# A graph network on one core: deeper rings in the edge sort, three banks of sums and fewer waits in the layers

## What is computed

```python
for l in range(3):
    X = einsum('ne,ref->rnf', out, weights[l])        # one product per edge type
    msg = X[edge_type, dst] + biases[l][edge_type]
    out = segment_sum(msg, src)                        # relu after layers 0 and 1
x = layernorm(x + out)
alpha = beta * cos(x[row], x[col])                     # row, col: the edges and loops
x = layernorm(x + softmax over each row's edges of alpha, times x[col])
```

## Time and profile before

| quantity | before |
|---|---|
| median of 3 runs | 4264.41 us |
| the profiled execution | 4270.03 us |
| its span, first to last instruction | 4268.3 us |
| mean granted TensorE clock | 0.862 of full speed |
| TensorE matmul busy | 3096.6 us (73%) |
| VectorE busy | 2434.5 us (57%) |
| ScalarE busy | 857.6 us (20%) |
| GpSimd busy | 2752.9 us (64%) |
| instructions | 55641 |

### The profile page before, as it was taken

The page is one execution under the profiler, slowest core; times in us unless marked ns, Lnnn a source line. Parts: engine busy times, 40 slices in busy tenths (PEclk is TensorE's granted clock), DMA queues, the critical chain, the costliest instruction groups (busy, mean ns, idle before and its releaser), DMA issues.

```text
span 4268.3 us, 55641 instructions
## 1 busy us (share of the span) xinstructions
PE 3096.6 (73%) x13925; PEld 1821.7 (43%) x13926; DVE 2434.5 (57%) x9103; ACT 857.6 (20%) x1992; POOL 2752.9 (64%) x2839
## 2 busy tenths in 40 slices
PE   7799957676776678667667667777775655656998
PEld 4455424333433334333334333344333434434776
DVE  9888855554555556555554554465554333335999
ACT  2599801001001000001001001001000000002665
POOL 0777777777777772777777777647777777772000
PEclk9899979999899997999998998898997555556999
DMA  4100013333433437333333333553433222224564
GB/s 157 42 2 2 2 45 83 78 71 80 80 72 78 81 72 175 70 72 76 83 72 74 84 74 71 71 175 76 83 72 85 53 53 53 53 53 76 185 192 141
DMA packets 377130, 343.02 MB, mean 80 GB/s; under 512 B 263666, under 2 KB 327722, under 8 KB 376712
## 3 DMA queue, kind: packets, MB, share of 16 engines
q0 software_dynamic: 90368, 165.49, 19.7%
q1 hardware_dynamic: 83112, 113.25, 8.0%
q10 hardware_dynamic: 203360, 60.73, 5.9%
HBM read 232.12 MB, written 107.13 MB: 79 GB/s over the span
## 4 chain that ended last, share of the span: by engine, by line
POOL 63%; issue 21%; PE 9%; DVE 5%; DMA 2%; ACT 1%; SPq 0%; POOLq 0%; DVEq 0%; ACTq 0%
POOL region L817 55%; POOL scattered_edges L800 8%; PE ps L958 2%; PE ps L929 2%; PE ps L986 2%; DMA region<-x_of_type,arrays 1%; DVE region L340 1%; DVE region L608 1%; PE ps L961 1%; PE ps L919 1%; DVE region L580 0%; PE ps L908 0%; DVE arrays L368 0%; DVE arrays L379 0%; DVE region L599 0%
## 5 line engine op out<-in xcount | busy, mean ns | idle before, releaser
L817 POOL DMA_INDIRECT region<-x_of_type,arrays x2520 | 2415.7, 959 | 918.9 <-issue 764.9
L908 PE MATMUL ps<-oh,region 128*128 128x102 f32 x5040 | 1261.3, 340 | 725.9 <-DMA region<-x_of_type,arrays 707.0
L441 DVE TENSOR_SCALAR oh<-iota_w,arrays 128x102 f32<-128x102 f32 x2528 | 724.3, 290 | 1703.7 <-PE ps L908 1701.4
L919 PE MATMUL ps<-region 128*128 128x510 f16 x4200 | 1402.0, 410 | 346.8 <-issue 195.8
L908 PEld LDWEIGHTS ps<-oh,region 128*128 128x128 f32 x5040 | 1000.1, 228 | 1454.9 <-DMA region<-x_of_type,arrays 1281.2
L919 PEld LDWEIGHTS ps<-region 128*128 128x128 f16 x4200 | 434.5, 113 | 549.8 <-issue 527.2
L505 DVE TENSOR_TENSOR region<-region,ps 128x102 f32 x2520 | 646.1, 256 | 3.6 <-issue 3.2
L1048 ACT COPY region<-ps 128x510 f32<-128x510 f32 x155 | 89.8, 579 | 2482.8 <-PE ps L919 2482.3
L800 POOL DMA_INDIRECT scattered_edges<-region x304 | 332.8, 1095 | 207.0 <-DVE ends L398 109.3
L887 PE MATMUL ps<-region 128*128 128x420 f16 x2016 | 362.6, 342 | 24.9 <-ACT region L1025 24.9
L1025 ACT ACTIVATE region<-region 128x128 f16<-128x128 f16 x1008 | 348.8, 394 | 39.7 <-DVE region L418 29.6
(11 more groups left out here) (173 smaller groups left out, 1486.4 us busy)
## 6 DMA issues: line engine op xcount, KB each, us to landing
region<-x_of_type,arrays POOLq DMA_INDIRECT x2520, 2.6
edge_counts<-region ACTq DMA_DIRECT2D x155, 255.0 KB
arrays<-edge_counts SPq DMA_DIRECT2D x40, 960.0 KB, 5.0
x_of_type<-region SPq DMA_DIRECT2D x50, 576.0 KB, 3.9
edge_absent<-region ACTq DMA_DIRECT2D x155, 127.5 KB
region<-edge_absent SPq DMA_DIRECT2D x40, 480.0 KB, 4.4
x_of_type<-x0st SPq DMA_DIRECT2D x51, 192.0 KB, 1.8
scattered_edges<-region POOLq DMA_INDIRECT x304
```

What stands on the lines that cost most here:

```text
L441: ins = nc_.tensor_scalar(oh[:, t % U, 0:RB], iota_r, rowf[:, t % NT:t % NT + 1], None, ALU.is_equal)
L817: pool.indirect_dma_start(out=grow[:, t % GR, :], out_offset=None, in_=xt, in_offset=bass.IndirectOffsetOnAxis(ap=gix[:, t:t + 1], axis=0) ...
L908: mm = pe.matmul(ps[:, 6 + n % 2, t * RB:(t + 1) * RB], grow[:, u % GR, :], oh[:, u % U, 0:RB], start=True, stop=True)
L919: mm = pe.matmul(ps[:, c, 0:CW], cl[:, q % CR, c * P:(c + 1) * P], cr[:, q % CR, :], start=False, stop=False, skip_group_check=True)
```

## The change

In the sort the rings get `KR` = 28 places, in a larger stretch of `region` that is free by then, and `s_put` is raised once per `KS` = 14 columns; VectorE and ScalarE wait on it only every 14 columns. In the layers, the sums of four tiles go to three banks in turn instead of two, the tiles' one-hots lie in a ring of 12 (`ohr`, now in `region`) instead of 8, and the keys' one-hots in a ring of 8 instead of 5. TensorE reads the thresholds of five columns at once, and waits once per column, ahead of bank 0, for all five refilled banks. The last 12 one-hots past the end, which nobody uses, are no longer made. What is computed, and every compute instruction else, is the same.

```diff
-KR = 4
+SUMS = 3
+OH = 12
+KR = 28
+KS = 14
-    CR = 5
+    CR = 8
+    CL = 5
-        used[0] = NK * ET // 2
+        used[0] = max(GR * D, NP) + NP
+        ohr = part(OH * P).rearrange("p (u d) -> p u d", u=OH)
-            dve.sem_inc(s_add, 2 * SLOTS)
+            dve.sem_inc(s_add, SUMS * SLOTS)
             # the sort, VectorE (ScalarE's wait changes alike)
-                if t >= KR:
-                    dve.wait_ge(s_put, t - KR + 1)
+                if t >= KR and t % KS == 0:
+                    dve.wait_ge(s_put, (t - KR) // KS + 1)
-            dve.wait_ge(s_put, EP)
+            dve.wait_ge(s_put, EP // KS)
-                ins = nc_.tensor_scalar(oh[:, t % U, 0:RB], iota_r, ...
+                ins = nc_.tensor_scalar(ohr[:, t % OH, 0:RB], iota_r, ...
-            for u in range(U):
+            for u in range(OH):
                 one_hot(u)
...
-                    one_hot(first + i * BODY + u + U)
+                    if first + i * BODY + u + OH < NT * L:
+                        one_hot(first + i * BODY + u + OH)
-                    dve.wait_ge(s_add, i * BODY + (first + u + 2 * SLOTS))
+                    dve.wait_ge(s_add, i * BODY + (first + u + SUMS * SLOTS))
-                    nc_.tensor_tensor(h, h, ps[:, 6 + n % 2, t * RB:(t + 1) * RB], ALU.add).then_inc(s_add, 1)
+                    nc_.tensor_tensor(h, h, ps[:, 5 + n % SUMS, t * RB:(t + 1) * RB], ALU.add).then_inc(s_add, 1)
             # TensorE in the sort
-                mm.then_inc(s_put, 1)
+                if t % KS == KS - 1:
+                    mm.then_inc(s_put, 1)
             # TensorE in the layers
-                    mm = pe.matmul(ps[:, 6 + n % 2, ...], grow[:, u % GR, :], oh[:, u % U, 0:RB],
+                    mm = pe.matmul(ps[:, 5 + n % SUMS, ...], grow[:, u % GR, :], ohr[:, u % OH, 0:RB],
                         if c == 0:
-                            ready = values_of(pe, b7, k, CG * (MB - 1) + 1, 1)[0]
+                            if q % CL == 0:
+                                ready = values_of(pe, b7, k // CL, CG * (MB - 1) + 1, CL)
                             pe.wait_ge(s_co, k + 1)
-                        if c % 2 == 0:
-                            reg_wait(pe, s_cz, ready + min(c + 1, CG - 1))
-                        mm = pe.matmul(ps[:, c, 0:CW], cl[:, q % CR, c * P:(c + 1) * P], cr[:, q % CR, :],
+                            reg_wait(pe, s_cz, ready[q % CL] + (CG - 1))
+                        mm = pe.matmul(ps[:, c, 0:CW], cl[:, k % CR, c * P:(c + 1) * P], cr[:, k % CR, :],
```

More of the change, by code:

```diff
@@ L77, in gnn_program @@
     assert all(b * JOINT_MUL >> BLOCK_SHIFT == b // JB for b in range(NB))
-    assert CP <= REST and EP % U == 0 and U == 2 * KR and HW <= 512 and NT <= 1 << DIGIT
-    assert BODY == GR and GR % U == 0 and BODY % U == 0 and U == 2 * SLOTS and ET <= KW and NT % SLOTS == 0
+    assert CP <= REST and EP % KR == 0 and KR % KS == 0 and HW <= 512 and NT <= 1 << DIGIT
+    assert BODY == GR and GR % U == 0 and BODY % OH == 0 and BODY // SLOTS % SUMS == 0 and NT // SLOTS % SUMS == 0 and U == 2 * SLOTS and ET <= KW and NT % SLOTS == 0
     assert R * NP < 1 << ROW_BIT and RB <= P and ROW_BIT + 7 <= 2 * DIGIT and NB % JB == 0 and PAD_ROW <= NP
@@ L95, in gnn_program @@
     CB = 10
-    CR = 5
+    CR = 8
+    CL = 5
     CTURNS = -(-NT // CB)
     CQ = CTURNS * CB
-    assert (L - 1) * TURNS < CTURNS < L * TURNS and CB % CR == 0 and CQ + CR < KW
+    assert (L - 1) * TURNS < CTURNS < L * TURNS and CB % CL == 0 and CQ + CR <= KW
     PARTS = [[] for _ in range(BODY)]
@@ L440, in one_hot @@
             def one_hot(t):
-                ins = nc_.tensor_scalar(oh[:, t % U, 0:RB], iota_r, rowf[:, t % NT:t % NT + 1], None, ALU.is_equal)
+                ins = nc_.tensor_scalar(ohr[:, t % OH, 0:RB], iota_r, rowf[:, t % NT:t % NT + 1], None, ALU.is_equal)
                 if t % SLOTS == SLOTS - 1:
@@ L501, in take_tiles @@
                             cell_hots(i * CB + (CB * TURNS * l + q + CR - 1))
-                    dve.wait_ge(s_add, i * BODY + (first + u + 2 * SLOTS))
+                    dve.wait_ge(s_add, i * BODY + (first + u + SUMS * SLOTS))
                     h = hA[:, bass.ds(bs[t], RB)]
-                    nc_.tensor_tensor(h, h, ps[:, 6 + n % 2, t * RB:(t + 1) * RB], ALU.add).then_inc(s_add, 1)
+                    nc_.tensor_tensor(h, h, ps[:, 5 + n % SUMS, t * RB:(t + 1) * RB], ALU.add).then_inc(s_add, 1)
             for l in range(L):
                 if l:
-                    dve.wait_ge(s_add, NT * l + 2 * SLOTS)
+                    dve.wait_ge(s_add, NT * l + SUMS * SLOTS)
                     for n in range(XN):
@@ L907, in use_tiles @@
                         pe.wait_ge(s_add, i * BODY + (first + u + SLOTS))
-                    mm = pe.matmul(ps[:, 6 + n % 2, t * RB:(t + 1) * RB], grow[:, u % GR, :], oh[:, u % U, 0:RB],
+                    mm = pe.matmul(ps[:, 5 + n % SUMS, t * RB:(t + 1) * RB], grow[:, u % GR, :], ohr[:, u % OH, 0:RB],
                                    start=True, stop=True)
@@ L941, in _ @@
             pe.wait_ge(s_cz, CG + CG * MB)
-            pe.wait_ge(s_add, NT * L + 2 * SLOTS)
+            pe.wait_ge(s_add, NT * L + SUMS * SLOTS)
             turn(lambda b: hA[:, b * P:(b + 1) * P])
@@ L1021, in _ @@
                 act.wait_ge(s_hot, t + 1)
-                if t >= KR:
-                    act.wait_ge(s_put, t - KR + 1)
+                if t >= KR and t % KS == 0:
+                    act.wait_ge(s_put, (t - KR) // KS + 1)
                 for d in range(2):
```

## The result

The changed kernel has a median of 4239.87 us (4237.43 to 4242.11, 4 runs), against 4264.88 us (4263.59 to 4267.21) for the kernel before, measured in turn with it. The ratio is 0.9941, with a 95% interval from 0.9923 to 0.9958. The forecast was 4247.4 us, its range 4233 to 4271; the change is 25 us where 17 were forecast. The profiled execution took 4240.06 us, its span is 4238.3 us.

The account below looks back on a forecast made before the run. The prediction took GpSimd's row of indirect DMAs to bound the kernel, in the sort's scatter and the layers' gathers. Its terms, -22 + 3 + 2 = -17 us against 4264.41, gave 4247.4 us, with a range of 4233 to 4271.

Parts of the forecast that it names:

- What bounds the kernel: Whole kernel: GpSimd's indirect DMAs, 304 in the sort and 840 per layer; the scatter decides the sort's end.
- TensorE in the sort: 0.713 us per column stays: Sort, TensorE: one signal per 14 columns buys nothing; 504 columns keep ending at about 523.3 us.
- GpSimd freed by bursts, d = 0.04: Sort: GpSimd's wait d per issue within VectorE's bursts is 0.04 us; last scatter starts at about 510, against 544.19.
- The cap: End of sort: TensorE's half becomes the limit, L452 starts at 526 instead of 549.41, -23 us; -22 taken.
- The rule of the Trainium skill: Sort, against the step: each issue held for a whole burst, +203 us, 4472 us; chance 0.03 for full blocking.
- The four casts: Before the sort's columns: an issue took 2.36 us, until 0.12 us after the last cast; cited for the full blocking.
- The layers' rhythm, +3: Layers: contact with VectorE, 0.018 us per gather issue, may shift its phase; bounds -38 and +38 us, +3 taken.
- The end of layer 0, +2: End of layer 0: the single wait for all five banks delays the last tiles, +2 us.
- The sum: Whole kernel: -22 (sort) + 3 (layers' rhythm) + 2 (end of layer 0) = -17 us, 4247.4 us forecast.

Follow-up runs that it names:

- run with 310 columns: Changed kernel with 310 columns scattered by GpSimd and 498 placed by TensorE, instead of 304 and 504: 4237.79 us, ratio 0.9924 to the kernel before.
- run with the layers' part alone: Changed kernel with the sort's part taken back (ring of 4, a signal per column): 4265.99 us against 4269.40 for the kernel before, ratio 0.9992.
- six kernels named above: Kernel before; it with the sort's part alone, that with signals per 1, 2 or 4 columns; it with a fifth matmul: first to last gather 3323.1 to 3326.4 us.
- three kernels: Layers' part alone, the changed kernel, and it with 310 scattered columns: 3318.6, 3319.7 and 3321.3 us from layer 0's first gather to layer 2's last.
- columns of 0.89 us: Kernel before with a fifth matmul per column of the sort into a bank that nobody reads: 4337.60 us.
- last runs: Kernel before, changed kernel and it with 310 columns again, on one chip: 5137.34, 5117.56, 5119.41 us; changed kernel with short key comparisons, two chips: 5119.48, 5112.86 us.

## Why the prediction was right, point by point

- **What bounds the kernel.** Right. The layers' gathers did not move by more than 1.8 us in any layer, although TensorE was idle by other amounts and its mean granted clock fell from 0.862 to 0.825. The scatter was the end of the sort, and TensorE's half is now.
- **TensorE in the sort: 0.713 us per column stays.** Right: 155 matmuls in 27.82 us, so (27.82 - 0.34) / 154 = 0.178 us each.
- **GpSimd freed by bursts, d = 0.04.** The outcome is right: with work waiting at VectorE, GpSimd's issue falls to 0.96 us, so d was 0. The picture of a burst was not. The prediction let GpSimd drift through VectorE's comparisons and be caught now and then. In its place stands a lock in which VectorE waits, 0.2 us per two columns, so that VectorE's 0.56 us per column in a burst was 0.63. I had 510 for the last scatter and 507.19 came. The time does not test this step finely, since any start before 520.8 gives the same end of the sort: that a wrong picture of the burst cost nothing is owed to the cap.
- **The cap.** Right in kind, short by 1.0 us: L457 at 524.98 against 526. Of this, 0.7 us is TensorE's last matmul, which ended at 522.6 and not at 523.3. The term was -22, one below my own cap of 23, and measured -24.4. The run with 310 columns confirms that TensorE's half is this cap.
- **The rule of the Trainium skill** (page "SBUF — State Buffer", section "Who interferes with whom") is that of a VectorE instruction in a two-port mode and a GpSimd instruction the one that issues first gets the shared pair of ports for the whole instruction, and the other fully blocks. The reading of it that the prediction carried to its fullest, one issue blocked for a whole burst of comparisons, did not occur: right through the bursts the issues take 0.96 us. The four casts ahead of the sort did hold an issue for 2.36 us, and for 2.35 in the changed kernel; what sets them apart from the comparisons is not shown. That either engine can be the one that waits agrees with the rule. Which of them came second cannot be read from the starts: in both locks an issue starts while a wide comparison is under way (at 301.06 within 300.92 to 301.35 before, at 498.35 within 498.31 to 498.77 after), and yet the issue is lengthened in the one, and the next wide comparison in the other.
- **The layers' rhythm, +3.** It came out as -2.8 over the three layers (-0.6, -1.8, -0.4). My reason for +3 was that TensorE would be on time more often because it reads fewer registers. That misread the change: as many values are read, five at a time, and the matmuls' stops by it grew, as the run with the layers' part alone shows. The mean issue of layer 0 stayed at 0.963 us. The sign had no ground. By that run's ratio of 0.9992 (0.9983 to 1.0002) the effect can't be told from 0; the traces hint at about -5 for the layers' part as a whole.
- **The end of layer 0, +2.** Too large. The longer wait did come. The emptying of the banks and the relu in the changed kernel, which answer to the earlier trace rows:

```profile
1596.76 0.58 ACT L1055 COPY region<-ps 128x510 f32<-128x510 f32 x1 [78.34 <-PE ps L926]
...
1602.82 1.01 PE L926 MATMUL ps<-region 128*128 128x510 f16 x2 [5.00 <-ACT ps L1044]
...
1610.15 2.10 DVE L517 TENSOR_SCALAR hB<-region 128x640 f32<-128x640 f32 x5
```

  TensorE stood for 5.00 us until all five banks were refilled. But the emptying began at 1596.76, 3.5 us after the layer's last gather was issued (1593.3), where before it was 5.3 us (1623.58 against 1618.3). The relu comes 16.85 us after that gather, 16.7 before. The earlier emptying is not shown to be the change's alone, since TensorE's granted clock was 0.50 of full speed from 1610 to 1624 before, and 1.00 from 1593 to 1597 in the changed kernel. Other traces help. With the layers as before, the six kernels named above empty the first bank 4.3 to 5.3 us after the gather and start the relu after 15.6 to 16.7 us, 16.0 in the mean. With the new layers three kernels have 3.5 to 4.2 and 16.7 to 17.1, 16.9 in the mean. So the new layers cost about 1 us at this place and not 2. The time to the next layer's first gather, -0.9 in the table, is 69.5 to 72.9 us in the six and 71.7 to 72.2 in the three, so its sign says nothing.
- **The sum.** -22 + 3 + 2 = -17 stands against -24.4 - 5.6 = -30.0 in the profiled executions, and against -25 in the medians, as the profiled execution of the kernel before lay 5 us above its median. The forecast falls short by 2.4 us in the sort, and it gave +5 to the layers and what follows, where nothing or a few us less came. The sort's term carried it. The terms of the layers had no ground in the rows or were too large, and a forecast without them would have been nearer.

## What to carry to other kernels

When two engines meet at a shared resource at periods that nearly fit, look at the spacing of their starts, not at their busy shares: a lock makes one of them pay in every round. Which one pays depends on who has work waiting, so give slack, by a deeper ring with bundled signals, to the engine that can afford to wait, and let the one on the chain (the row of work that sets the end) run at its own pace. Here a deep ring alone was not enough, and neither was a bundle of two; a bundle of four was. After such a step the next bound is the other half of the work, so look whether shifting the split pays.

## What the runs showed of the hardware that I had not expected

- The lock has two stable forms with the same instructions: GpSimd at 1.12 us every 1.43 with VectorE undisturbed, or GpSimd at 0.96 us every 1.26 and VectorE's 840-column comparison at 0.64 instead of 0.43 us. With columns of 0.89 us there is a third, of two issues (1.11 and 0.96 us) to three columns.
- Reading five values into TensorE's registers at once came with stops of its matmuls of 2.3 us, reading one with stops of 0.4 us. Reading them together saved nothing.
- In the last runs TensorE started a matmul of the sort only every 2.8 us for long stretches, while VectorE, ScalarE and GpSimd kept their durations. Two matmuls that follow each other in the changed kernel there:

```profile
302.26 0.51 PE L893 MATMUL ps<-region 128*128 128x420 f16 x1 [2.29 <-issue]
...
305.06 0.51 PE L893 MATMUL ps<-region 128*128 128x420 f16 x1 [2.29 <-issue]
```

  TensorE's busy time by stretch (us, busy and matmuls, granted clock, DMA share, GB/s):

```profile
200.00:560.00 360.00, 80.29 (x207) 0.52 0.02 2
560.00:880.00 320.00, 318.04 (x1783) 1.00 0.00 1
```

  From about 542 us it was back at full pace. No run here tells what held it. It came on a chip that had run the kernel before in 4269.72 us earlier, and in the kernel before as well, to judge by its time.
